# A two-layer graph network on one core: weights asked for in half pieces paced by TensorE, with a lead of four, five and six pieces in place of six

## The reference

```python
h = maximum(layernorm(x), 0)
# layer 0: attention with 16 heads of 64 under a mask made from the edges
q = h @ wq.T + bq; k = h @ wk.T + bk; v = h @ wv.T + bv
q2 = q @ wiq.T + biq; k2 = k @ wik.T + bik; v2 = v @ wiv.T + biv
x = x + softmax(q2 k2^T / 8 + mask) v2 @ wo.T + bo
# layer 1: a relational graph convolution with 8 relations, then a gate
h = maximum(layernorm(x), 0)
u = h @ root + bias + sum_r mean_r(h[src]) @ weight[r]
z = concat([u, h]) @ w_gate + b_gate
x = x + tanh(u) * z + h * (1 - z)
```

## Time and profile before

| what | value |
|---|---|
| time, median of 3 runs | 228.63 us |
| the three runs | 226.9, 228.63, 232.76 us |
| the profiled execution | 230.86 us |
| its span in the trace | 228.7 us |
| granted TensorE clock over the span | 1.0 |
| PE busy (share of the span) | 217.3 us (95%) |
| DVE, ACT, POOL busy | 80.5, 22.3, 24.6 us |
| read from HBM | 75.97 MB |

### The profile page before, as it was taken

The page is one execution under the profiler, slowest core; times in us unless marked ns, Lnnn a source line. Parts: engine busy times, 40 slices in busy tenths (PEclk is TensorE's granted clock), DMA queues, the critical chain, the costliest instruction groups (busy, mean ns, idle before and its releaser), DMA issues.

```text
span 228.7 us, 10049 instructions
## 1 busy us (share of the span) xinstructions
PE 217.3 (95%) x4797; PEld 210.8 (92%) x4797; DVE 80.5 (35%) x138; ACT 22.3 (10%) x41; POOL 24.6 (11%) x53
## 2 busy tenths in 40 slices
PE   1999998999999999999999999999999999999894
PEld 1889998999999999799989999999999888999893
DVE  2459838051499731457466500000000000000614
ACT  2523000000020120313051000000000000000001
POOL 2255005400000000010003910000000000000000
PEclk9999999999999999999999999999999999999999
DMA  6999999999989989948981999999999999999202
GB/s 224 381 392 419 426 420 408 398 398 387 393 307 380 388 312 322 386 146 308 335 341 37 391 401 390 384 387 393 393 403 374 388 378 376 386 397 337 110 3 69
DMA packets 12363, 76.99 MB, mean 337 GB/s; under 512 B 2554, under 2 KB 2818, under 8 KB 3108
## 3 DMA queue, kind: packets, MB, share of 16 engines
q1 hardware_dynamic: 11792, 75.95, 85.9%
q10 hardware_dynamic: 532, 0.42, 0.6%
HBM read 75.97 MB, written 0.39 MB: 334 GB/s over the span
## 4 chain that ended last, share of the span: by engine, by line
PE 94%; DMA 2%; issue 1%; DVE 1%; ACT 0%
PE acc L779 81%; PE acc L1026 4%; DMA x_sb<-in_x 2%; PE turn L967 1%; PE side L827 1%; PE side L967 1%; PE side L1026 1%; PE turn L855 1%; DVE stats L504 1%; PE acc L797 1%; PE turn L797 0%; PE turn L871 0%; PE side L838 0%; PE turn L838 0%; PE acc L871 0%
## 5 line engine op out<-in xcount | busy, mean ns | idle before, releaser
L779 PE MATMUL acc<-mean,raw 128*64 128x96 f32 x2048 | 85.5, 246 | 1.4 <-issue 1.4
L779 PEld LDWEIGHTS acc<-mean,raw 128*64 128x64 f32 x2048 | 84.9, 137 | 1.8 <-issue 1.8
L779 PE MATMUL acc<-hT,raw 128*64 128x96 f32 x1024 | 44.7, 247 | 0.2
L779 PEld LDWEIGHTS acc<-hT,raw 128*64 128x64 f32 x1024 | 42.9, 137 | 1.5 <-issue 1.2
L742 DVE TENSOR_TENSOR uT<-acc,uT 128x384 f32<-128x384 f32 x2 | 1.1, 558 | 83.0 <-PE acc L779 83.0
L779 PE MATMUL acc<-qT,raw 128*64 128x96 f32 x512 | 22.0, 246 | 1.0 <-issue 1.0
L779 PEld LDWEIGHTS acc<-qT,raw 128*64 128x64 f32 x512 | 21.4, 137 | 1.3 <-issue 1.3
L779 PE MATMUL acc<-kT,raw 128*64 128x96 f32 x512 | 21.7, 246 | 0.0
L779 PEld LDWEIGHTS acc<-kT,raw 128*64 128x64 f32 x512 | 21.3, 137 | 0.3 <-issue 0.3
L779 PE MATMUL acc<-uT,raw 128*64 128x96 f32 x256 | 13.0, 271 | 0.0
L779 PEld LDWEIGHTS acc<-uT,raw 128*64 128x64 f32 x256 | 12.6, 156 | 0.3 <-ACT uT L408 0.2
(11 more groups left out here) (177 smaller groups left out, 149.7 us busy)
## 6 DMA issues: line engine op xcount, KB each, us to landing
raw<-in_weights SPq DMA_DIRECT2D x136, 512.0 KB, 5.6
raw<-in_weights SPq DMA_DIRECT2D x4, 1024.0 KB, 9.8
x_sb<-in_x SPq DMA_DIRECT2D x1, 192.0 KB, 3.7
x_sb<-in_x ACTq DMA_DIRECT2D x1, 192.0 KB, 3.8
out<-out_rows SPq DMA_DIRECT2D x1, 192.0 KB, 2.1
out<-out_rows ACTq DMA_DIRECT2D x1, 144.0 KB, 2.2
out<-out_rows SPq DMA_DIRECT2D x1, 48.0 KB, 2.5
bias_rows<-in_biases ACTq DMA_DIRECT2D x1, 36.0 KB
```

The source lines that it names most:

```text
L779: mm = pe.matmul(a[g * HD:(g + 1) * HD, b, c * N:(c + 1) * N], raw[:, s, at:at + HD], moving(k0 + k), start=opens and k0 == 0 and c == 0 a ...
```

## The change

A piece is still two transfers of 512 KB, but each has its own wait. The first half of piece n is asked for when PE has used piece n - lead(n); the second half when PE is half through piece n - lead(n) + 1, told by a new semaphore `step_used`, which the last matmul of a piece's second output chunk raises (c = 1 of 0 to 3). lead(n) is 4 pieces for n below 32, 5 for n from 32 to 38, and 6 from 39 on; before it was 6 throughout. The ring keeps its six places. The first four pieces are one transfer each without a wait, as before; pieces 4 and 5, which were asked for at once before, now wait. The pieces of the last matrix don't raise `step_used`.

```diff
+STEPS = 2
 def transfers(n):
-    return 1 if n < 4 else 2
+    return 1 if n < lead(n) else STEPS
+
+def lead(n):
+    return 4 if n < 32 else 5 if n < 39 else SLOTS
...
             def fetch(n):
                 where = PIECES * SEQUENCE[n // PIECES] + kind_of(n)
-                if n >= SLOTS:
-                    sp.wait_ge(piece_used, n - SLOTS + 1)
                 for j in range(transfers(n)):
+                    if n >= lead(n) and j == 0:
+                        sp.wait_ge(piece_used, n + 1 - lead(n))
+                    if n >= lead(n) and j > 0:
+                        sp.wait_ge(step_used, (STEPS - 1) * (n + 1 - lead(n)) + j)
                     part = slice(j, P, transfers(n))
                     sp.dma_start(raw[part, n % SLOTS, :], weights[where, part]).then_inc(raw_landed[n % SLOTS], 16)
...
             def piece(n, moving, a, opens=True, closes=True):
...
+                    if c < CH - 1 and (c + 1) * STEPS % CH == 0:
+                        mm.then_inc(step_used, 1)
                 mm.then_inc(piece_used, 1)
```

More of the change, by code:

```diff
@@ L170, in gnn_kernel @@
         piece_used = sem("piece_used")
+        step_used = sem("step_used")
         consts_ready = sem("consts_ready")
```

## The result

The changed kernel takes 236.26 us (median of 4 runs, 234.33 to 236.6), the kernel before 229.57 (226.9 to 232.76): a ratio of 1.036 with an interval of 1.024 to 1.047. It is slower by over 2%. The forecast was 226.7 us, in a range up to 229.5.

A forecast was written before the change was run, and what follows sets the result against it. PE's matmul stream was taken as the bound, with stops waiting for its own instructions. From the profiled 230.86 us, -1.5 - 2.4 + 0.1 + 0.1 = -3.7 gave 227.2, or 226.7 us for the median run; range 225.3 to 229.5.

The forecast's parts named there:

- the time without stops: Whole kernel: the profiled execution of 230.86 us would take 226.2 us without any of PE's stops, 4.65 us together.
- (a): Start: with four pieces asked for, the backlog ends by about 16 us and the stops at 30 and 36 go, -1.5 us.
- the sign that (a) is wrong: In the profile after, the stops near 30 and 36 us stay although landing is short.
- first rival: Instruction loads don't wait for the weight backlog, so lead and half steps change nothing: 228.6 us, or 229.0; chance 0.22.
- (b): Five late stops: a later second half leaves one half ahead of an instruction load; -2.4 us, bounds -3.15 and +1.0.
- (c): Pieces below 39: the shorter lead leaves some 1.9 us of margin; one hiccup, +0.1 us, bounds 0 and +5.
- second rival: Pieces 4 to 12: PE starves on lead four as landing exceeds 6.6 us, losing 5.0 us: 233.6 us; chance 0.07.
- (d): PE's matmuls: 68 added increments of `step_used`, one a piece, cost +0.1 us, at most 0.45.

The follow-up runs named there:

- the two cut kernels: The kernel before and the changed kernel, each without weights from piece 40 on: 227.61 us (ratio 0.998) and 227.67 us (one execution, no ratio).
- the late pair: Kernel before, second half of each piece asked for one piece later, with the next piece's first half: 230.7 us against 229.34, too wide for an interval.

## Why the prediction was wrong

What bounds the kernel was read rightly: PE's stream with stops where an instruction load comes late, all else free. The runs without late weights show that, and the time without stops, 226.2 forecast, is 226.1 in both profiled executions. It was the sign of one term that failed.

(a) The start, -1.5 us: right in kind. Landing from 20 to 34 us fell from 8.0 to 5.9, and with the lead alone the early stops fell from 1.75 to 0.52 us, -1.2. In the full change the gain was eaten by the half steps: 3.51 us of early stops, with those near 30 and 36 us still there (0.64 and 0.61 us) although landing had become short. I had named that as the sign that (a) is wrong and the first rival holds; the sign was wrong, since the lead alone removes both.

(b) The half steps, -2.4 us with +1.0 as the upper bound: this is the step that failed. I had the load wait for what was asked for ahead of it, so that a second half sent behind the block's begin would be out of its way and 3.5 us become 2.3. In the block of 180.4 this order came about, and the load still took 3.4 us or more. What I had wrong is that only one half would lie ahead: three lay there, 1.6 MB, since halves asked for long before had not been moved yet, and at some 400 GB/s three halves would be 3.9 us. The rows had told it: the earlier trace rows has 1.23 MB moved ahead of a load that I gave 1.05 MB to wait for. Measured alone, the half steps cost +2.3%, some 5 us (3.4 us by the two medians), in place of -2.4. My bound against me, +1.0, allowed for a few loads shifted into bad places, not for every load losing.

(c) The short lead, +0.1: near, with 0.37. The margin was thinner than the 1.9 us I had left, since landing took 5.9 us from 20 to 34 us and 5.8 from 44 to 58, in place of the 4.7 that I had read behind a pause (the kernel before has 5.5 from 44 to 58): pieces 5, 6 and 7 had 0.06, 0.25 and 0.43 us between landing and start. PE's waits for weights came to 0.07 + 0.30 us. The second rival, PE starving on lead four, stayed at that; it shows only with four issues a piece.

(d) The increment, +0.1: nothing that the run could show, 0.9995.

The first rival (the load's delay has nothing to do with the weights' queue) is refuted by the two cut kernels. The rule that spoke for it, the Trainium skill's "DMA: Bandwidth & Descriptors", section "Queues, rings and completion order", lets an engine change between queues at packet boundaries. If one transfer's share of an engine is the packet, 1.25 us for 512 KB, that forbids delays of 3 us; those are measured. But no run shows what a packet is for these transfers, so this doesn't refute the rule. It has a point which I set aside: what a load waits for is a lump, so the lump's size matters. The runs agree in direction: 1 MB 2.0% slower, 512 KB sent singly 2.3 to 3.8% slower, 256 KB with rows of 8 KB and lead six -0.1 to +0.6%, sent singly or together.

Why 512 KB together costs nothing and singly costs is shown in its effect, not in its mechanism. With pairs, many loads start within about 1 us of their block's begin: six of the first nine late ones in the kernel before, and most in the runs with the increments alone and the late pair. With single half pieces, in the changed kernel and with the steps alone, none of the 16 is under 1.4 us. My reading is that the weights' queue on an engine runs dry for a moment after each pair and a load goes at once, while evenly sent halves leave no such moment and it goes after whole transfers, by the bytes moved 1.3 to 3.2 of them. Much speaks against it: four small transfers at once had no dry moments by their delays; the pairs of 512 KB at the middle of a piece had none either, no load under 2.0 us; and ahead of the early load at 128.0 us the weights' queue was at 104.9%.

A rival is that a load takes its turn in the order of asking, with a lag. Over the 269 loads from 128 us on in the 17 traces with all weights and a full DMA rate, what was moved between a block's begin and its load goes with what had been asked for over 1.1 us before that begin and not moved (correlation 0.69; the lag is fitted to the same loads). But it misses the comparison that matters: of eight halves issued 0.9 to 1.1 us ahead of a block in the changed kernel six were moved ahead of the load, of sixteen pairs issued 0.95 to 1.03 us ahead with the increments alone none was. So the mechanism stays open, and no run was made for this rival.

What the ramps of the lead add (1.036 against 1.023) is open too: landing rises to 8 us where the lead goes from five to six, near 130 us, and three stops follow there, but the kernel with lead five can't be told from either.

By the ratios no variant that computes the whole beats the kernel before by more than 0.5%; that one is the lead alone, both halves together.

## What to carry to other kernels

When DMA runs near its limit, PE's own instruction loads are one more customer of the same engines, and a long unrolled stream stops in steps of 128 matmuls with "issue" ahead of the gap; look at when each instruction load starts in its block before explaining such stops otherwise. Before crediting a load with a shorter wait, count the bytes that are asked for and not yet moved, not only the last issue. Pacing transfers evenly with their use isn't neutral, and it cost most here when a transfer was 512 KB. Try a smaller transfer at the same moments, and count the issues, since SP at 0.6 us each can become the next limit.

## What the runs showed of the hardware

- Without weight traffic an instruction load starts with its block (within 0.6 us); behind it, 0.4 to 4.6 us later. Up to about 2.9 us PE doesn't stop; beyond, the stop is nearly what the delay has over that (0.71 us at 180.2 in the kernel before, by a load 3.5 us or more late). The Trainium skill's "Runtime: NRT & Kernel Launch", section "Instruction fetch mechanics", calls the crossing of a block mostly hidden: so it is with free DMA engines, and not here, with 10.1 us of 236.6.
- 512 KB transfers into 64 adjacent partitions, in place of every second one, bring the whole stream to some 230 GB/s at full DMA share, from some 400.
- An issue on SP takes a median of 0.47 us (changed kernel) to 0.54 us (before) for 512 KB transfers and 0.59 us for 256 KB ones.
- Two executions of one kernel can differ by 2% in little but these stops: the kernel with the lead alone took 225.9 us with 0.53 us of them, and 230.65 with 5.45.
